# Context attention: K's fp16 parts made from normed rows in SBUF and turned by DMA instead of on TensorE, with new cyclic orders

## What is computed

```python
q = _ln((x @ Wq + bq).reshape(b, s1, H, HD), qn_w, qn_b)          # H = 16 heads, HD = 32
kv = jnp.concatenate([y_main @ Wk + bk, y_main @ Wv + bv], axis=-1)
kv = kv.reshape(b, s2, H, 2 * HD)
k = _ln(kv[..., :HD], kn_w, kn_b)
v = kv[..., HD:]
ctx = _attn(qT, k.transpose(0, 2, 1, 3), v.transpose(0, 2, 1, 3))  # softmax(q k^T / sqrt(32)) v
```

## Time and profile before

| | |
|---|---|
| median of 3 runs | 3381.3 us (3379.84 to 3383.14) |
| profiled execution: its own time, first to last instruction | 3386.0 us |
| TensorE busy over the span | 3119.5 us, 92% |
| VectorE | 2655.1 us, 78% |
| ScalarE | 2269.3 us, 67% |
| GpSimd | 1864.8 us, 55% |

### The profile page before, as it was taken

The page is one execution under the profiler, slowest core; times in us unless marked ns, Lnnn a source line. Parts: engine busy times, 40 slices in busy tenths (PEclk is TensorE's granted clock), DMA queues, the critical chain, the costliest instruction groups (busy, mean ns, idle before and its releaser), DMA issues. The chain is left out here.

```text
span 3386.0 us, 89189 instructions
## 1 busy us (share of the span) xinstructions
PE 3119.5 (92%) x35753; PEld 1945.5 (57%) x35753; DVE 2655.1 (78%) x4082; ACT 2269.3 (67%) x4027; POOL 1864.8 (55%) x2294
## 2 busy tenths in 40 slices
...
GB/s 121 61 34 23 23 33 24 32 23 33 23 34 23 28 114 125 109 184 278 302 305 128 92 22 33 23 34 23 33 23 34 23 23 33 23 21 54 1 68 25
DMA packets 102368, 223.67 MB, mean 66 GB/s; under 512 B 35445, under 2 KB 47861, under 8 KB 96202
## 3 DMA queue, kind: packets, MB, share of 16 engines
...
## 5 line engine op out<-in xcount | busy, mean ns | idle before, releaser
L307 POOL TENSOR_TENSOR a_elo<-a_e 128x1024 f16<-128x1024 f32 x428 | 867.3, 2026 | 160.6 <-ACT a_e L384 159.6
L545 PE MATMUL a_ps_k<-l_wk,a_yh 128*128 128x512 f16 (+1 forms) x1664 | 568.3, 382 | 31.4 <-DVE a_yl L411 27.4
L545 PE MATMUL a_ps_v<-l_wv,a_yh 128*128 128x512 f16 (+1 forms) x1664 | 568.0, 382 | 19.1 <-DVE a_v L439 19.1
L450 DVE TENSOR_REDUCE a_mx<-a_ps_m 128x2 f32<-128x1024 f32 x384 | 466.7, 1215 | 13.0 <-PE a_ps_m L583 12.8
L382 ACT ACTIVATE a_e<-a_ps_t 128x1024 f32<-128x1024 f32 x428 | 410.9, 960 | 98.2 <-PE a_ps_t L617 91.8
L287 POOL TENSOR_TENSOR a_khat<-a_kc,a_rstd 128x512 f32<-128x512 f32 (+1 forms) x416 | 443.7, 1073 | 16.5 <-PE a_ps_kt L566 6.0
L384 ACT ACTIVATE a_e<-a_ps_t 128x1024 f16<-128x1024 f32 x428 | 410.7, 960 | 0.0
L411 DVE TENSOR_TENSOR a_yl<-l_land,a_yh 128x256 f16<-128x256 f32 (+1 forms) x416 | 352.0, 847 | 19.3 <-ACT a_yh L335 19.0
L418 DVE SCALAR_TENSOR_TENSOR a_kc<-a_ps_k,l_bk 128x512 f32<-128x512 f32 (+1 forms) x416 | 284.0, 683 | 91.6 <-PE a_ps_k L545 91.2
L641 PE MATMUL a_ps_o<-a_v,a_e 128*128 128x65 f16 (+1 forms) x3240 | 344.6, 194 | 10.4 <-POOL a_elo L307 10.4
L432 DVE SCALAR_TENSOR_TENSOR a_kl<-a_ps_kt,a_kh 128x512 f16<-128x512 f32 (+1 forms) x416 | 274.1, 659 | 91.2 <-ACT a_kh L356 91.2
...
## 6 DMA issues: line engine op xcount, KB each, us to landing
...
l_land<-in_ctx SPq DMA_DIRECT2D x32, 768.0 KB, 4.7
...
qs_dram<-p_q SPq DMA_DIRECT2D x32, 128.0 KB, 2.4
dca_dram<-p_od SPq DMA_DIRECT2D x16, 256.0 KB, 2.4
a_q<-qs_dram SPq DMA_DIRECT2D x32, 128.0 KB, 2.0
```

Of the source, the lines that this page charges most:

```text
L307: pool.tensor_tensor(rest[0:r, :, 0:w], full[0:r, :, 0:w], high[0:r, :, 0:w], ALU.subtract)\
L450: dve.tensor_reduce(mx[:, g, :, c], ps_m[:, :, :], AX.X, ALU.max).then_inc(mx_done, 1)
L545: m = pe.matmul(out[0:r, :], part[:, t, c, 0:r], w[:, wpart, c, :], start=(c == 0 and a == 0), stop=(c == KC - 1 and a == 2))
```

## The change

`kh` and `kl` no longer read turned K from PSUM. ScalarE now makes the high part directly from `khat` (rows on partitions) into the left half of a new buffer `khl` of two slots, and VectorE makes the low part from `khat` and that high part into the right half. Then one DMA from SyncE's queue turns the 128 x 1024 fp16 values of both parts, 256 KB, into `kk`, which holds `kh` and `kl` as views. TensorE's transposes, their PSUM bank and the semaphore `kt_done` are gone. The waits move with it: `hat` of tile i waits for `kl` of tile i-2, `kh` of tile i waits until the DMA of tile i-2 has landed, and the products of TensorE that read `kh` or `kl` wait for the landing of the DMAs. SyncE's stream has a turn for each tile in it, and the loads of the context and the queries stand between the turns. The last tile is turned as 64 rows. All five order tables are new.

```diff
+            kk = sb("kk", [P, 2, 2 * GROUPS, KCOLS], F16)
+            kh, kl = kk[:, :, 0:GROUPS], kk[:, :, GROUPS:2 * GROUPS]
+            khl = sb("khl", [P, 2, 2 * D], F16)
...
+        def wait_turned(eng, tiles):
+            for k in range(2):
+                n = len(range(k, tiles, 2))
+                if n:
+                    eng.wait_ge(turned[k], 16 * n)
...
+                def turn(b, i):
+                    n, r = b * KT + i, -(-rows(i) // 64) * 64
+                    sp.wait_ge(kl_done, n + 1)
+                    sp.dma_start_transpose(kk[:, b % 2, :, i * P:i * P + r], khl[0:r, n % 2, :]).then_inc(turned[n % 2], 16)
...
+                for b in range(B):
+                    for i in range(KT):
+                        if i == 3 and b + 1 < B:
+                            sp.wait_ge(yl_done, b * KT + YA)
+                            load_a(b + 1)
+                        if i == 10 and b + 1 < B:
+                            sp.wait_ge(yl_done, b * KT + KT)
+                            load_b(b + 1)
+                        turn(b, i)
+                    if b >= 1 and b + 1 < B:
+                        sp.wait_ge(q1_done, b)
+                        load_q(b + 1, (b + 1) % 2)
...
                 def hat(at, i):
-                    need(pool, kt_done, n - 1)
+                    need(pool, kl_done, n - 1)
...
                 def k_high(at, i):
-                    act.wait_ge(kt_done, n + 1)
-                    act.activation(kh[:, at.nbp, :, i * P:i * P + r], ps_kt[:, :, 0:r], ACT.Identity, bias=one[:, 0:1])\
+                    act.wait_ge(hat_done, n + 1)
+                    if n >= 2:
+                        act.wait_ge(turned[n % 2], 16 * (n // 2))
+                    act.activation(khl[0:r, n % 2, 0:D], khat[0:r, tile_par(at.nbp, i), :], ACT.Identity, bias=one[0:r, 0:1])\
...
                 def k_low(at, i):
-                    dve.scalar_tensor_tensor(out=kl[:, at.nbp, :, i * P:i * P + r], in0=ps_kt[:, :, 0:r], scalar=1.0,
-                                             in1=kh[:, at.nbp, :, i * P:i * P + r], op0=ALU.add, op1=ALU.subtract)\
+                    dve.scalar_tensor_tensor(out=khl[0:r, n % 2, D:2 * D], in0=khat[0:r, tile_par(at.nbp, i), :], scalar=1.0,
+                                             in1=khl[0:r, n % 2, 0:D], op0=ALU.add, op1=ALU.subtract)\
...
-                def k_turned(at, i):
-                    for g in range(GROUPS):
-                        m = pe.transpose(ps_kt[:, g, :], khat[:, t, g * P:(g + 1) * P], ident[:, :])
-                    m.then_inc(kt_done, 1)
...
                 def first_scores(at, m):
-                    pe.wait_ge(kh_done, at.nb * KT + min(4 * c + 4, KT))
+                    wait_turned(pe, at.nb * KT + min(4 * c + 4, KT))
...
                 def scores(at, j):
-                        pe.wait_ge(kl_done, at.b * KT + KT)
+                        wait_turned(pe, at.b * KT + KT)
...
-    DVE: vl10- kl7- m3- yl12- rd11- kl8- m4- vl11- kc12- m5- rd12- kl9- yl0 m6- yl1 kl10- m7- kc0 vl12- kl11-
+    DVE: kc12- kl9- m4- yl0 rd12- vl12- m5- kl10- kl11- m6- yl1 kc0 m7- yl2 kc1 m8- kl12- m9- rd0 m10- vl0
```

More of the change, by code:

```diff
@@ L31 @@
 TAIL = MAIN - (KT - 1) * P
-KCOLS = MAIN + MAIN % 2
+KCOLS = -(-MAIN // 64) * 64
 NCH = -(-MAIN // 512)
@@ L48 @@
 ORDER = """
[L49 to L57, removed]
-    DVE: vl10- kl7- m3- yl12- rd11- kl8- m4- vl11- kc12- m5- rd12- kl9- yl0 m6- yl1 kl10- m7- kc0 vl12- kl11-
-    DVE: m8- rd0 m9- vl0 yl2 kc1 m10- vl1 yl3 m11- kc2 rd1 m12- t- vl2 kc3 qs- yl4 kl12- ql- vl3 yl5 rd2 kc4
@@ L60 @@
-    DVE: rd3 o1- vl4 yl6 kc5 kl0 rd4 vl5 rd5 kl1 yl7 kc6 vl6 kl2 rd6 kc7 yl8 vl7 kl3
-    POOL: hat4- lo3- hat5- lo4- nw3- lo5- hat6- lo6- hat7- lo7- nw4- lo8- hat8- lo9- hat9- lo10- nw5- hat10-
-    POOL: lo11- hat11- lo12- lo13- nw6- hat12- qm nw0 hat0 hat1 lo0 nw1 lo1 hat2 hat3 lo2 nw2
+    PE: k7- pv2- v7- s4- k8- v8- pv3- m0- s5- k9- v9- pv4- m1- s6- k10- s7- m2- pv5- v10- k11- pv6- s8- v11-
+    PE: pv7- s9- m3- k12- v12- m4- pv8- s10- m5- k0 pv9- s11- m6- v0 pv10- m7- s12- k1 m8- pv11- s13- m9-
@@ new lines @@
+    PE: pv12- m10- pv13- k2 m11- v1 m12- tb- v2 k3 s0 v3 k4 s1 v4 k5 s2 pv0 v5 pv1 k6 s3 v6
+    ACT: vh3- yh5- kh0- sq3- e1- sq4- vh4- kh1- yh6- r1- e2- vh5- sq5- yh7- kh2- e3- vh6- r2- kh3- sq6- yh8-
+    ACT: sq7- vh7- yh9- e4- kh4- vh8- r3- kh5- yh10- sq8- e5- vh9- yh11- sq9- e6- kh6- r4- kh7- e7- vh10-
+    ACT: yh12- sq10- kh8- e8- sq11- vh11- e9- kh9- r5- sq12- yh0 vh12- yh1 e10- kh10- r6- kh11- e11- yh2 e12-
+    ACT: kh12- sq0 e13- vh0 vh1 yh3 sq1 qh- vh2 yh4 r0 sq2 e0
+    DVE: rd4- vl5- yl7- kc6- rd5- kl2- vl6- kc7- kl3- yl8- rd6- vl7- rd7- kc8- yl9- kl4- vl8- m0- rd8- kl5-
@@ new lines @@
+    DVE: kc9- yl10- vl9- m1- rd9- kl6- yl11- kc10- kl7- m2- vl10- o0- kc11- yl12- rd10- kl8- rd11- vl11- m3-
+    DVE: kc12- kl9- m4- yl0 rd12- vl12- m5- kl10- kl11- m6- yl1 kc0 m7- yl2 kc1 m8- kl12- m9- rd0 m10- vl0
+    DVE: m11- kc2 m12- t- vl1 qs- yl3 rd1 ql- vl2 kc3 yl4 rd2 vl3 yl5 kc4 rd3 kl0 o1- vl4 kl1 yl6 kc5
+    POOL: lo4- nw3- hat6- hat7- lo5- lo6- nw4- hat8- lo7- hat9- lo8- lo9- nw5- hat10- hat11- lo10- nw6- lo11-
+    POOL: hat12- lo12- lo13- nw0 hat0 hat1 lo0 qm lo1 nw1 hat2 lo2 hat3 lo3 nw2 hat4 hat5
@@ L130, in context_attention @@
         ps_v = ps("ps_v", [P, 512])
-        ps_kt = ps("ps_kt", [P, GROUPS, P])
         ps_m = ps("ps_m", [P, 2, 512])
@@ L142, in context_attention @@
         newton = [sem(f"newton{j}") for j in range(5)]
-        kt_done, kh_done, kl_done = sem("kt_done"), sem("kh_done"), sem("kl_done")
+        kh_done, kl_done = sem("kh_done"), sem("kl_done")
+        turned = [sem("turned0"), sem("turned1")]
         vh_done, vl_done = sem("vh_done"), sem("vl_done")
```

18 lines of the change are left out of this document (removed).

## The result

The changed kernel takes 3466.2 us, median of 4 runs (3464.8 to 3479.0), against 3382.2 us for the kernel before in the same session: ratio 1.025, 95% interval 1.0237 to 1.0264. It is slower; the forecast was 3350 us and faster, and its range ended at 3455.

What follows compares the result with a forecast made beforehand. TensorE bounds the kernel at 67.3 of 68.5 us per batch; VectorE would replace it, period 67.2. Steady batches -40 us, fill +8, so 3381.3 - 32 = 3349, say 3350 us; range 3290 to 3455.

Steps and rivals of the forecast that it cites:

- What a bound VectorE leaves idle: VectorE, as the new bound, keeps 1.5 of its 8.9 us idle time per batch; period 67.2 us.
- rival B: VectorE keeps half its idle time, 4.5 us, through late handoffs from TensorE and ScalarE: period 70.2 us, 3440 us; 23%.
- The price of a `kl`: On VectorE each full-tile `kl` waits 0.51 us for GpSimd, `yl`'s own mean: 6.1 us more per batch.
- That two SBUF inputs cost VectorE the time: `kl` with both inputs in SBUF and GpSimd's SBUF reads exclude each other; VectorE becomes the bound at 65.7 us.
- That GpSimd has room: GpSimd, busy 51.1 us per batch and sometimes held up by a `kl`, has 17 us of room.
- Rival E: `kl` mostly misses GpSimd, waiting 0.2 us each; VectorE needs 62.0 us per batch, time 3240 us; 12%.
- The ceiling of 8.1 us per batch: Removing the transposes frees 8.1 us per batch on TensorE, to 59.3 us; at most 242 us in all.
- ScalarE's `kh`: Read from SBUF, `kh` takes 0.631 instead of 0.686 us, 0.7 us less per batch on ScalarE; no effect on time.
- The DMAs: On SyncE's queue each turn lands in about 3 us (bounds 2 and 12), in time for its readers, costing nothing.
- Rivals C and D: Turns land late at `m8`, 3410 to 3470 us, 13%; turns themselves are the bound, 3670 us or beyond 6000, 7%.
- `m0`, to which it gave more than 6 us: Tile 3's turn comes behind a 4.7 us load on SyncE's queue; `m0` needs it more than 6 us later.
- Fill: In each attention's first batch the last turn's landing delays `m12` and `s0`: 4 us each, 8 together (-10 to +20).

Runs made afterwards that it cites:

- e4: The changed kernel with three matmuls that nothing reads added on TensorE ahead of each of `m7` to `m10`: 3436.9 us, ratio 1.0147.
- e10: The changed kernel with only 4 of the 12 matmuls per tile in the products for K and V: 3481.4 us, ratio 1.0271.
- e14: The changed kernel with a second PSUM buffer for V's product: 3472.6 us, ratio 1.0266.
- e1: The changed kernel, `kl` reading a constant PSUM tile instead of the high part in SBUF, so it comes out as zero: 3282.0 us, ratio 0.9703.
- e2: The kernel before, `kl` reading two SBUF tiles and coming out as zero, `hat` waiting for `kl` of tile i-2: 3522.4 us, ratio 1.0409.
- e3: The kernel before without TensorE's transposes for all tiles but the first: 3326.9 us, ratio 0.9823.
- e12: The kernel before with 416 turning DMAs of a constant buffer added on SyncE's queue, next batch's q load ahead of tile 3's turn: 3387.4 us, ratio 0.999.

## Why the prediction was wrong

**The failed step is "What a bound VectorE leaves idle": "of its present idle time ... I leave 1.5".** It is 4.8 us. VectorE's busy time came out as 66.4 against 65.7 us; with 1.5 us idle the period would have been 67.9 and the time about 100 us less. These 3.3 us x 30 are 100 of the 123 us by which the profiled span misses its forecast (3477.2 against 3386 - 32 = 3354). It is rival B in size (4.5 us, period 70.2, 3440), and the wait rows look like its mechanism: ScalarE and TensorE, each in a fixed order, come late for VectorE. Of it the runs showed that 1.3 us of the period, 1.0 of them idle time, are TensorE's half clock behind its own waits (e4), which no step of the prediction had; that less work on TensorE doesn't remove the rest (e10, with the clock as a reservation), nor a second buffer for V's product (e14). What would remove the remaining 3.8 us was not found. That it is the fixed orders is argued from the waits, not shown.

**The price of a `kl`: right in kind, mis-sized.** The step "I take 0.51, `yl`'s own mean" measured 1.478 - 0.679 = 0.80 us, 3.5 us per batch more. The prediction named the tie itself, that GpSimd's next entry is a `lo` or a `hat`, and took `yl`'s mean all the same: three of four `kl`s began within a `lo`. The last tile, costed at nothing, takes 1.71 us against 0.35 (not shown before: it had 196 columns, now 512 on 49 rows), 1.4 more. Both were made up by `yl`, which lost 12 x (0.927 - 0.541) = 4.6 us: I had left its share as it was, though the exclusion is a matter of the order and the order was new. That VectorE's busy time came out right is luck, errors that cancel.

**That two SBUF inputs cost VectorE the time: right** (e1, e2). The rule of the Trainium skill, SBUF — State Buffer, section Who interferes with whom, was weighed in the prediction for this: the two engines exclude each other for whole instructions. The traces agree, 2.31 us for a `kl` begun inside a `lo`, and 0.68 in e1 with a PSUM operand; in the kernel before, 34 `kl`s begun inside a `lo` from 400 to 840 us took 0.69 each. And GpSimd pays as well, as the prediction said, 56.9 us per batch against 51.4 in e1. **That GpSimd has room: right**, it still does nothing for 14.4 us per batch, and its longest wait, 11.9 us, is for `r` of the next batch. **Rival E** asked for a `kl` that misses GpSimd; e1 is what it would be worth.

**The ceiling of 8.1 us per batch: wrong by the overlap**, 4.9 in e3; TensorE came out at 62.7 us, not near 60. **ScalarE's `kh`: wrong in sign**, 0.72 us from SBUF (L371, 300.1 us for 416) against 0.686 from PSUM, 0.4 us per batch on an engine that has room.

**The DMAs: right but for one wait.** 3 us taken, 3.1 measured; `m8` doesn't wait; e12 shows nothing lost. Rivals C and D fall. What the prediction had wrong is `m0`, to which it gave more than 6 us: the turn of tile 3, behind the context load, holds TensorE up ahead of `m0` in four of the 11 batches from 300 to 1100 us, 0.2 to 1.0 us each, while VectorE is busy with a `kl`. The figure of the Trainium skill, VectorE: DVE Perf Modes, section The three transpose paths, from which the prediction took an estimated 10.5 us a turn, doesn't carry over to eight blocks in one DMA: the median is 3.1. With the sentence of the Trainium skill, Advanced Engine Details and Errata, section X-Bar Transpose, that such DMAs are as fast as others, the trace agrees nearly: 3.1 us for 256 KB, beside 2.0 for a plain store of 256 KB and 2.4 for one of 128 KB.

**Fill: about as forecast**, 91 - 81 = 10 us against 8. How they are shared between the first batches and the last ones was not taken apart.
